# Attention in a gated cross-attention block: a three-bank score ring with one maximum per bank, a four-bank key ring, and the fold and all sums in one block

## What is computed

```python
# x: (4, 1024, 512), ctx_768: (4, 2048, 384), all fp32; 16 heads of width 32
def xattn(query, key_value, ...):
    q = (query @ Wq + bq)...; k = (key_value @ Wk + bk)...; v = (key_value @ Wv + bv)...
    attn = jnp.einsum('bhqd,bhkd->bhqk', q, k) * D ** (-0.5)
    attn = jax.nn.softmax(jnp.clip(attn, -10000., 10000.), axis=-1)
    return jnp.einsum('bhqk,bhkd->bqhd', attn, v).reshape(B, Nq, Cq) @ Wo + bo
x = x + tanh(g_xattn) * xattn(layernorm(x), ctx_768, ...)
x = x + tanh(g_ffn) * ffn(layernorm(x), ...)     # a second layernorm, fc1, silu, fc2, dequantized weights
```

## Time and profile before

| | us |
|---|---|
| median of three runs | 3081.51 (3080.73 to 3082.74) |
| the profiled execution | 3078.93 |
| its span, first to last instruction | 3077.1 |
| PE busy | 2964.0 |
| DVE busy | 2148.1 |
| ACT busy | 1631.7 |
| POOL busy | 1837.3 |

### The profile page before, as it was taken

How to read it: one execution, slowest core, us unless ns; L and a number is a source line. 1 busy time by engine, 2 the same in 40 slices (tenths; PEclk the granted TensorE clock), 3 DMA queues, 4 the chain that set the end, 5 groups by cost and what they waited for, 6 DMA issues and landing times. The chain is left out here.

```text
span 3077.1 us, 50977 instructions
## 1 busy us (share of the span) xinstructions
PE 2964.0 (96%) x14950; PEld 1784.3 (58%) x14950; DVE 2148.1 (70%) x3149; ACT 1631.7 (53%) x2968; POOL 1837.3 (60%) x887
## 2 busy tenths in 40 slices
PE   8999979999999999999999999999969799999999
PEld 6888754444444444444444444444436577777777
DVE  5555557777777777777777777777646787777775
ACT  3222226666666666666666666666621344444443
POOL 4655638888888888888888888888853000000000
PEclk9999979999999999999999999999989899999999
DMA  6666752222222212221222222122168200000000
GB/s 206 227 223 229 230 183 58 47 62 62 50 53 62 61 44 60 62 58 45 62 62 53 51 62 61 47 58 62 24 177 267 109 28 28 28 22 20 22 20 28
DMA packets 144977, 255.26 MB, mean 83 GB/s; under 512 B 22066, under 2 KB 63090, under 8 KB 137716
## 3 DMA queue, kind: packets, MB, share of 16 engines
q1 hardware_dynamic: 144884, 254.13, 29.2%
HBM read 162.32 MB, written 91.23 MB: 82 GB/s over the span
## 5 line engine op out<-in xcount | busy, mean ns | idle before, releaser
L844 DVE TENSOR_REDUCE at_half_max<-ps 128x1 f32<-128x1024 f32 x1024 | 1216.6, 1220 | 463.3 <-PE ps L672 457.6
L791 ACT ACTIVATE at_probT<-ps 128x512 f32<-128x512 f32 x2048 | 1058.0, 603 | 455.2 <-PE ps L691 455.1
L584 POOL TENSOR_TENSOR at_gp_sum<-at_gp_sum,at_probT 128x1024 f32<-128x1024 f32 x512 | 1218.0, 2379 | 42.3
L672 PE MATMUL ps<-k_stack,q_stack 96*128 96x512 f32 x2048 | 706.5, 427 | 14.4 <-issue 11.9
L691 PE MATMUL ps<-q_stack,k_stack 98*128 98x512 f32 x2048 | 656.6, 402 | 2.1 <-ACT at_probT L791 2.1
L672 PEld LDWEIGHTS ps<-k_stack,q_stack 96*128 96x128 f32 x2048 | 349.5, 191 | 490.9 <-issue 324.0
L725 PE MATMUL ps<-at_probT,v_head 128*32 128x512 f32 x4096 | 492.5, 598 | 0.9 <-ACT at_probT L791 0.9
L691 PEld LDWEIGHTS ps<-q_stack,k_stack 98*128 98x128 f32 x2048 | 385.0, 188 | 175.8 <-ACT at_probT L791 106.4
L579 POOL TENSOR_TENSOR at_gp_sum<-at_probT 128x1024 f32<-128x1024 f32 x128 | 306.2, 2392 | 267.0 <-ACT at_probT L791 267.0
L1396 POOL TENSOR_TENSOR x_keep<-x_keep,b_half 128x2048 f32<-128x2048 f32 x8 | 37.5, 4686 | 555.2 <-DVE x_keep L1419 555.2
L1449 DVE SCALAR_TENSOR_TENSOR ff_acc<-ps,s_t,ff_acc 128x512 f32<-128x512 f32 x384 | 288.1, 750 | 20.6 <-DVE ff_acc L1449 0.9
(11 more groups left out here) (171 smaller groups left out, 3444.0 us busy)
## 6 DMA issues: line engine op xcount, KB each, us to landing
k_stack<-kT_hi SPq DMA_DIRECT2D x128, 256.0 KB, 4.9
kT_hi<-pi_out_hi SPq DMA_DIRECT2D x16, 1024.0 KB, 4.4
kT_lo<-pi_out_lo SPq DMA_DIRECT2D x16, 1024.0 KB, 6.7
v_heads<-pi_v_out SPq DMA_DIRECT2D x16, 1024.0 KB, 10.4
q_stack<-qT_hi SPq DMA_DIRECT2D x128, 128.0 KB, 3.4
k_stack<-kT_lo SPq DMA_DIRECT2D x64, 256.0 KB, 4.2
v_head<-v_heads SPq DMA_DIRECT2D x64, 256.0 KB, 5.1
pi_c_in<-in_ctx_dram SPq DMA_DIRECT2D x16, 768.0 KB, 9.9
```

What stands on the lines that cost most here:

```text
L584: pool.tensor_tensor(gp_sum[lane % 2][:, :, :], gp_sum[lane % 2][:, :, :], pairs[:, 2 * i + 2:2 * i + 4, :], ALU.add).then_inc(gp_added, 1)
L672: mm = pe.matmul(ps[:, n, :], q_stack[buf][0:PARTS, rows], k_stack[buf][0:PARTS, BANK * n:BANK * (n + 1)], start=True, stop=True)
L791: act.activation(probT[lane % 2][:, kv, :], src, ACT.Exp).then_inc(exp_done, 1)
L844: dve.tensor_reduce(dst, src, AX_X, ALU.max).then_inc(max_done, 1)
```

## The change

Banks: scores use banks 0 to 2 as a ring over single score tiles, and keys use banks 3 to 6 as a ring of four; bank 7 stays. Each score matmul now signals by itself and waits for the maximum of the tile three before it. DVE takes one maximum for each bank (512 columns), four a step where there were two, and `split_maxima` reads four columns for each tile. SUMS moves from lag 13 to 14, so that `fold_values` and `last_sums` are issued one behind the other in one step of the unit, and the step at lag 13 has no narrow block. The rest of the diff is the clipping path.

```diff
--- before.py
+++ after.py
@@ -489,18 +489,21 @@
     STEPS = N_HEADS * PER_HEAD
     UNITS = N_HEADS * HALVES
     KVT = SK // P
-    TURN, KEYS, PV, SUMS, FOLD = 7, 8, (11, 12), 13, 14
+    TURN, KEYS, PV, SUMS, FOLD = 7, 8, (11, 12), 14, 14
     TAIL = FOLD + 1 - QT
-    RING = 3
+    RING, SCORE_BANKS = 4, 3
     SPLITS = 6
     GP_ADDS = 5
     PARTS = 3 * D
     assert SK == 4 * BANK and HALVES == 2 and KVT == 16
 
-    assert BODY * KVT % RING == 0
+    assert BODY * KVT % RING == 0 and 4 * UNROLL % SCORE_BANKS == 0
 
     def key_bank(lane, kv):
-        return 4 + (KVT * lane + kv) % RING
+        return SCORE_BANKS + (KVT * lane + kv) % RING
+
+    def score_bank(slot, n):
+        return (4 * slot + n) % SCORE_BANKS
 
     def unit_at(base, slot, lag):
 
@@ -515,7 +518,7 @@
         k_stack, q_stack, v_head = H["k_stack"], H["q_stack"], H["v_head"]
         probT = [sb(f"probT{i}", [P, KVT, BANK]) for i in range(2)]
         gp_sum = [sb(f"gp_sum{i}", [P, 2, BANK]) for i in range(2)]
-        half_max = sb("half_max", [P, BODY * QT, 2])
+        half_max = sb("half_max", [P, BODY * QT, 4])
         row_max = sb("row_max", [P, QT])
         neg_pair = sb("neg_pair", [P, QT, 2])
         neg_lo = sb("neg_lo", [P, QT, 1])
@@ -642,7 +645,7 @@
 
                 for half in range(HALVES):
                     sp.wait_ge(stored[half], 64 * EARLY)
-                sp.wait_ge(max_done, 2 * STEPS)
+                sp.wait_ge(max_done, 4 * STEPS)
                 for i in range(3):
                     sp.dma_start(early_sums[i], sum_d[i][0:EARLY, :].rearrange("h (a n) -> (h a) n", n=BANK)) \
                         .then_inc(sums_in, 16)
@@ -666,13 +669,11 @@
                 rows = slice(P * (slot % PER_HEAD), P * (slot % PER_HEAD + 1))
                 if n == 0 and slot % PER_HEAD == 0:
                     pe.wait_ge(qk_loaded[buf], 96 * base + 96)
-                if n % 2 == 0:
-
-                    need(pe, max_done, 2 * (s - 1) + n // 2 + 1)
-                mm = pe.matmul(ps[:, n, :], q_stack[buf][0:PARTS, rows],
+
+                need(pe, max_done, 4 * s + n - SCORE_BANKS + 1)
+                mm = pe.matmul(ps[:, score_bank(slot, n), :], q_stack[buf][0:PARTS, rows],
                                k_stack[buf][0:PARTS, BANK * n:BANK * (n + 1)], start=True, stop=True)
-                if n % 2:
-                    mm.then_inc(score_done, 1)
+                mm.then_inc(score_done, 1)
 
             def keys(base, slot, i):
 
@@ -832,13 +833,13 @@
             by_path(act, act_steps)
 
         def dve_steps(dve, clipping):
-            def maxima(slot, s, half):
-                dve.wait_ge(score_done, 2 * s + half + 1)
-                dst = half_max[:, slot, half:half + 1]
-                src = ps[:, 2 * half:2 * half + 2, :].rearrange("p b n -> p (b n)")
+            def maxima(slot, s, n):
+                dve.wait_ge(score_done, 4 * s + n + 1)
+                dst = half_max[:, slot, n:n + 1]
+                src = ps[:, score_bank(slot, n), :]
                 if clipping:
-                    need(dve, max_done, 2 * s + half)
-                    dve.tensor_scalar(clipped[:, :], src, A["clip_high"][:, 0:1], None, ALU.min, ALU.max,
+                    need(dve, max_done, 4 * s + n)
+                    dve.tensor_scalar(clipped[:, 0:BANK], src, A["clip_high"][:, 0:1], None, ALU.min, ALU.max,
                                       accum_out=dst).then_inc(max_done, 1)
                 else:
                     dve.tensor_reduce(dst, src, AX_X, ALU.max).then_inc(max_done, 1)
@@ -851,21 +852,22 @@
                 n = SPLITS * unit
                 half = slot // QT % HALVES
                 pair = half_max[:, first:first + QT, :]
-                dve.wait_ge(max_done, 2 * QT * (unit + 1))
+                dve.wait_ge(max_done, 4 * QT * (unit + 1))
                 need(dve, split_done, n)
                 if clipping:
-                    dve.scalar_tensor_tensor(row_max[:, :], pair[:, :, 0], A["clip_low"][:, 0:1], pair[:, :, 1],
-                                             ALU.max, ALU.max).then_inc(split_done, 1)
+                    dve.tensor_scalar(pair, pair, A["clip_low"][:, 0:1], None, ALU.max).then_inc(split_done, 1)
                     dve.wait_ge(split_done, n + 1)
+                    dve.tensor_reduce(row_max[:, :], pair, AX_X, ALU.max).then_inc(split_done, 1)
+                    dve.wait_ge(split_done, n + 2)
                     need(dve, row_turned, unit)
                     dve.tensor_scalar(neg[:, 0:QT], row_max[:, :], -1.0, None, ALU.mult).then_inc(split_done, 1)
-                    dve.wait_ge(split_done, n + 2)
+                    dve.wait_ge(split_done, n + 3)
                     dve.scalar_tensor_tensor(neg[:, QT:2 * QT], row_max[:, :], -1.0, neg[:, 0:QT].bitcast(F32),
                                              ALU.mult, ALU.subtract).then_inc(split_done, 1)
-                    dve.wait_ge(split_done, n + 3)
-                    for part in range(2):
-                        dve.tensor_copy(wide[:, part, :, :], neg[:, QT * part:QT * (part + 1)].bitcast(F32).unsqueeze(2)
-                                        .to_broadcast([P, QT, P])).then_inc(split_done, 1)
+                    dve.wait_ge(split_done, n + 4)
+                    dve.tensor_copy(wide[:, :, :, :].rearrange("p w t n -> p (w t) n"),
+                                    neg[:, 0:2 * QT].bitcast(F32).unsqueeze(2).to_broadcast([P, 2 * QT, P])) \
+                        .then_inc(split_done, 1)
                 else:
                     dve.tensor_reduce(neg_pair[:, :, 0], pair, AX_X, ALU.max, negate=True).then_inc(split_done, 1)
                     dve.tensor_reduce(neg_pair[:, :, 1].bitcast(F32R), pair, AX_X, ALU.max).then_inc(split_done, 1)
@@ -899,10 +901,12 @@
                 s = at(base, slot, 0, UNROLL, STEPS)
                 if s is not None:
                     maxima(slot, s, 0)
+                    maxima(slot, s, 1)
                 shift(base, slot, 0)
                 shift(base, slot, 1)
                 if s is not None:
-                    maxima(slot, s, 1)
+                    maxima(slot, s, 2)
+                    maxima(slot, s, 3)
                 split_maxima(base, slot)
                 shift(base, slot, 2)
                 shift(base, slot, 3)
```

## The result

The changed kernel takes 3295.99 us (median of 4 runs, 3293.56 to 3297.43) against 3082.12 for the kernel before in the same comparison: a ratio of 1.0693, 95% interval 1.068 to 1.0706. It is slower, as forecast, but by 214 us where 40 were forecast, and it lies far above the range, 3070 to 3165.

A forecast was written before the change was run, and what follows sets the result against it. PE's stream was taken to bound the attention stage. Per unit -0.24 - 0.49 + 0.19 + 0.19 + 0.71 = +0.36 us, times 124 +44, the rest -4: 3121.5 us against a median of 3081.51, range 3070 to 3165.

The forecast's parts named there:

- What bounds the kernel, and the unit as the measure: Attention stage: PE's stream sets the time of a unit (one head, half its queries); 14.46 us against 14.10, times 124.
- Scores in a ring of three, one maximum per bank: DVE's score maxima: 512-column reductions take 0.69 us, 0.60 apart; DVE's work per unit rises to 10.5, under PE's 14.
- a fall of the granted clock: PE's clock: named as making the prediction wrong if it fell with the new pauses, adding time; no size given.
- Scores gate the long stretch: PE's eight-score stretch without the fold block: scores wait for DVE's maxima, 4.57 us against 3.86 without waits, +0.71 a unit.
- the recurrence: PE's stretches summed: score j needs reduction j - 3 plus 0.94; four scores take 2.17 us, eight 4.57.
- A gated weight load: PE's weight load that waits for a bank's reader no longer hides under the matmul before; it costs 0.19 us.
- Keys in a ring of four, -0.11 three times: PE's stretches: the fourth key no longer waits for the first key's exponential, so 3 x 0.11 us a unit go.
- One block, -0.24: PE's fold and last-sums blocks become one of 1.85 us (-0.14) with one narrow-to-wide exit fewer (-0.10); POOL wait costs nothing.
- the terms for the first steps and the tail, -4: Outside steady units: first steps -1 us, tail -2 to -3 us from two merges and the ring of four; -4 taken.
- rival 1: PE never waits for a maximum: gain of 0.57 us a unit, 3006.5 us; chance 0.12.
- rival 3: DVE starts each reduction only when the one before is over: unit 14.82 us, 3166.5 us; chance 0.08.
- Rival 2: Near the balance: quicker reductions or a gated load of 0.10 for 0.19; unit 14.0 to 14.25, centre 3081.5 us; chance 0.15.

The follow-up runs named there:

- a_shift: The changed kernel with 24 instructions of already-met waits put on DVE ahead of its attention loop; 3131.89 us, ratio 1.016.
- a_rings_only: The changed kernel with a_shift's shift of DVE's loop and SUMS back at lag 13 (fold and last sums in two blocks); 3119.58 us, ratio 1.0124.
- b_merge: The kernel before with SUMS at lag 14 alone (one block of fold and sums, rings and maxima as before); 3082.66 us, ratio 0.9998.
- r43_plain: The changed kernel with three key banks and four score banks, plus 24 never-run instructions that move DVE's loop; 3044.78 us, ratio 0.9877.
- b_inter: The kernel before with PE's order in each half step key, score, key, score instead of two scores, two keys; 3062.62 us, ratio 0.9937.
- a_pad256: The changed kernel with 256 never-run instructions on DVE at the end of the clipping path; 3296.42 us, ratio 1.0695.
- b_body2: The kernel before with 96 instructions of already-met waits in DVE's attention loop, making its body 266 instructions; 3186.5 us, ratio 1.0339.
- b_body_at61: b_body2 with 182 never-run instructions on DVE at the end of the clipping path; 3360.61 us, ratio 1.0904.

## Why the prediction was wrong in size

*What bounds the kernel, and the unit as the measure.* Right. The unit was forecast at 14.46 and is 14.50; without the pauses (a_shift) the changed kernel is 3131.9, 10 us over the forecast, inside the range and with the sign and the mechanism foreseen.

*The step that failed: "Scores in a ring of three, one maximum per bank".* It priced the 48 added reductions of each pass as time on DVE (16 x 0.60 + 0.92 a unit) and nothing else. That they are also instructions in a loop, with one instruction of register arithmetic for nearly each, was no term of the sum. The row that could have warned was on the page before: a queue that fetches instructions, 47 transfers. The missing term is 19 x 8.6 = 164 us. Nor did it help to name a fall of the granted clock as what could make the prediction wrong: I looked for it as a follow-up of pauses of 0.7 us, which by themselves leave the clock at 1.00 (a_shift, window 1000 to 2000), while behind the long pause, with PE idle for 4.79 us, it was 0.50.

*Scores gate the long stretch.* Right: a_rings_only, b_merge, r43_plain and a_shift all came out within 11 us of the recurrence, and their stretches within 0.02. One size in it was off. A gated weight load costs 0.12, not 0.19: the changed kernel's pair at 1408.50 is followed by its keys 0.59 later where 0.47 is free of waits.

*Keys in a ring of four, -0.11 three times.* Wrong. The 0.11 was read from the wait of a weight load that nearly fitted under the matmul before it; 0.09 of it is the entry to the narrow block, which stays. The changed kernel pays it at three entries instead of the waits that I had removed. The two errors have opposite signs and nearly cancel in the unit (0.09 more for each of three entries, about 0.07 less for the one gated load that counts in each of three stretches). That the unit came out within 0.04 is in part luck. It showed at once where only one of them applies, in b_inter (3062.6 for 3022).

*One block, -0.24.* The entry adds 0.09 to it, which makes -0.33 for a merge that nobody waits for; b_merge shows that somebody does. Where no pause came before (a_shift), the block did not wait for POOL in an ordinary unit, only in the last one (2.5 us). That cancels most of the gain that I gave the tail: 3082.1 + 50 is already a_shift's time, so the terms for the first steps and the tail, -4, did not come.

*The rivals.* No gates (rival 1) and reductions one after the other (rival 3) are both refuted by the rows: the long stretch is 4.57, and eight reductions in a row take 4.88 us, 0.60 apart:

```profile
1401.58 4.88 DVE L845 TENSOR_REDUCE at_half_max<-ps 128x1 f32<-128x512 f32 x8 [0.53 <-PE ps L674]
```

The prediction took rival 3's rule from half of a passage. The section that it names of the Trainium skill ("VectorE: DVE Perf Modes", The DRAIN you can't avoid) also says that a next operation that is not held starts earlier, and with that the rows agree. Rival 2's doubt about the gate was right (0.12, near its 0.10), but the entry, which it lacked too, made up for it. None of the rivals was about instructions, so the range could not hold the time.

## What to carry to other kernels

When an edit adds instructions to a long unrolled loop, count the loop body of each engine, waits and register arithmetic included. Here a body of 266 was harmless or cost 8.6 us a pass by its place, and instructions in front of it, never-run ones too, moved that place. The profile's row for the instruction queue tells which of the two it is. When buffers are short, try which reader needs the spare one: here it was worth 87 us to the maxima (0.69 us each) and nothing to the exponentials (0.60 us). A wait in the list of waits is a cost only if the distance of starts grows by it.

## What the runs showed of the hardware that I had not expected

- A DVE loop body of 266 instructions costs a pause of 4.9 to 6.6 us (the changed kernel and a_pad256) at each jump back or none, by its place alone (3131.9 us for a_shift, 3296.4 for a_pad256); code that is never executed moves that place (b_body2 3186.5, b_body_at61 3360.6).
- Behind such a pause TensorE's granted clock stays at 0.50 for more than 8 us; PE is idle 5.3 us a pass (busy 946.5 of 1000 us from 1000 to 2000, ten passes), and the loss is 8.6 us.
- Going from wide matmuls to 32-column ones costs 0.09 us (b_inter) and coming back 0.10, though the profile shows PE busy throughout.
- 16 instructions of waits on DVE that are already met take 1.44 us, 0.09 each (b_body2).
